# The convolution's sum leaves its PSUM bank through VectorE, half an image at a time, and 155 expert tiles run in place of 156

## What is computed

```python
def _L0_conv_ref(x, w1, b1, w2, b2, bias):
    avg = jnp.mean(x, axis=(2, 3))
    mx = jnp.max(x, axis=(2, 3))
    wt = softmax(((mx @ w2.T + b2) - (avg @ w1.T + b1)).reshape(b * c, 1, K, K), axis=1)
    y = conv_general_dilated(x, wt, feature_group_count=b * c) + bias
    return y + x
def _L0_ffn_ref(x, Wg, bg, W1, b1, W2, b2):
    top_w, top_i = top_k(xf @ Wg + bg, 2)
    w = softmax(top_w)
    for e in range(8):
        out += w[:, e] * (gelu(xf @ W1[e] + b1[e]) @ W2[e] + b2[e])
x = x + _L0_conv_ref(_ln_c(x), ...)
t = _to_tokens(x)
t = t + _L0_ffn_ref(_ln_t(t), ...)
```

## Time and profile before

| what | us |
|---|---|
| median of 3 runs | 1596.86 (1596.85 to 1596.99) |
| the profiled execution's span | 1597.2 |
| image phase, to the last routing row | about 570 |
| expert phase, first to last result | 625 to 1509 |
| last phase | 1510 to 1597 |

### The profile page before, as it was taken

The page is one execution under the profiler, slowest core; times in us unless marked ns, Lnnn a source line. Parts: engine busy times, 40 slices in busy tenths (PEclk is TensorE's granted clock), DMA queues, the critical chain, the costliest instruction groups (busy, mean ns, idle before and its releaser), DMA issues.

```text
span 1597.2 us, 45596 instructions
## 1 busy us (share of the span) xinstructions
PE 1476.3 (92%) x12254; PEld 1135.9 (71%) x12255; DVE 1379.2 (86%) x2725; ACT 1069.8 (67%) x2410; POOL 973.9 (61%) x1062
## 2 busy tenths in 40 slices
PE   5899999999998777999999999999999999999776
PEld 2344545454545426999999999999999999999654
DVE  2568888888888856999999999999999999999654
ACT  4577777777777415777777777777777777777400
POOL 1004556456545674777777777777777777777500
PEclk7999999999999757999999999999999999999866
DMA  4202122212121183111111111111111111110199
GB/s 136 80 27 67 60 76 66 68 58 79 62 69 50 41 141 74 43 44 44 47 47 45 42 38 47 44 47 41 47 47 41 49 43 47 47 44 8 39 403 399
DMA packets 62200, 115.77 MB, mean 72 GB/s; under 512 B 15551, under 2 KB 39259, under 8 KB 62154
## 3 DMA queue, kind: packets, MB, share of 16 engines
q1 hardware_dynamic: 37354, 62.28, 12.8%
q0 software_dynamic: 18176, 34.27, 6.9%
q10 hardware_dynamic: 6624, 18.69, 3.3%
HBM read 60.22 MB, written 58.61 MB: 74 GB/s over the span
## 4 chain that ended last, share of the span: by engine, by line
POOL 33%; issue 27%; PE 23%; ACT 7%; DMA 5%; DVE 3%; POOLq 1%; SPq 1%; ACTq 0%; DVEq 0%
POOL token_out L501 17%; PE psV L816 11%; POOL yt L496 7%; POOL xn L489 7%; DMA ye<-token_out 4%; PE psV L767 4%; ACT spent L597 3%; PE psT L801 2%; PE psA L758 2%; PE psG L803 2%; POOL rows_by_pair L471 2%; ACT cv L585 1%; ACT sq L553 1%; PE psV L995 1%; DMA stage<-in_L_ffn_W_dram 1%
## 5 line engine op out<-in xcount | busy, mean ns | idle before, releaser
L1309 DVE TENSOR_TENSOR gl<-g,gh 128x512 f16<-128x512 f32 x624 | 527.2, 884 | 13.3 <-ACT gh L701 6.2
L501 POOL DMA_INDIRECT token_out<-yt,rt x312 | 399.5, 1280 | 186.1 <-POOL yt L496 133.5
L471 POOL DMA_INDIRECT rows_by_pair<-rows,idx x256 | 271.7, 1061 | 322.0 <-issue 198.7
L816 PE MATMUL psV<-lp,diag 128*128 128x512 f32 x576 | 275.1, 610 | 18.7 <-ACT cv L585 17.6
L701 ACT ACTIVATE gh<-g 128x512 f16<-128x512 f32 x468 | 276.3, 624 | 17.2
L694 ACT ACTIVATE g<-psT 128x512 f32<-128x512 f32 x312 | 183.1, 597 | 107.3 <-DVE gl L1309 83.4
L694 ACT ACTIVATE g<-psV 128x512 f32<-128x512 f32 x312 | 185.1, 597 | 91.7 <-PE psV L935 80.7
L956 PE MATMUL psR<-wall,gh 128*128 x1248 | 222.7, 273 | 0.6 <-DVE ya L1326 0.6
L956 PE MATMUL psG<-wall,gh 128*128 x1248 | 222.7, 273 | 0.0
L957 PE MATMUL psG<-wall,gl 128*128 x1248 | 214.3, 219 | 0.0
L957 PE MATMUL psR<-wall,gl 128*128 x1248 | 214.3, 219 | 0.0
(11 more groups left out here) (210 smaller groups left out, 2951.6 us busy)
## 6 DMA issues: line engine op xcount, KB each, us to landing
rt<-rows_by_pair SPq DMA_DIRECT2D x156, 133.0 KB
xb<-in_x_dram SPq DMA_DIRECT2D x32, 512.0 KB, 3.5
ye<-token_out SPq DMA_DIRECT2D x32, 512.0 KB, 7.8
out_dram<-oe ACTq DMA_DIRECT2D x32, 512.0 KB, 8.5
token_out<-yt,rt POOLq DMA_INDIRECT x312
rows_by_pair<-rows,idx POOLq DMA_INDIRECT x256, 2.5
stage<-in_L_ffn_W_dram SPq DMA_DIRECT2D x1, 2048.0 KB, 8.6
rows_by_pair<-pad_rows SPq DMA_DIRECT2D x15, 133.0 KB
```

The source lines that it names most:

```text
L471: gp.indirect_dma_start(rows_dram, bass.IndirectOffsetOnAxis(ap=idx[p][:, b:b + 1].bitcast(U32), axis=0), rows[p][:, b, :], None).then_inc ...
L501: gp.indirect_dma_start(y_dram, bass.IndirectOffsetOnAxis(ap=rt[r][:, b, ID:ID + 1].bitcast(U32), axis=0), yt[r][:, b, :], None, bounds_ch ...
L816: ins = te.matmul(psConv.rearrange("p (h w) -> p h w", w=WW), diag[k][:, m, :], lp[j][:, y:y + HH // 2, dx:dx + WW], start=(m == 0), stop= ...
L1309: v.tensor_tensor(gl[side][q][:, cols], g[side][:, cols], gh[side][q][:, cols], ALU.subtract).then_inc(lo_done, 1)
```

## The change

`take` and the buffers `cv` are gone. `add_image` now works on half an image: it waits for the convolution's half (`conv_ready`), reads the bank, adds the bias (a value per partition) and the image in one instruction, writes half of `x1` and increments `cv_ready`, for which TensorE waits as before. The loads of images and the first `window` wait on `cv_ready` too, in place of `x_used`. There are four calls in a step where there were two: half 0 of image 0 behind `norm` 0, its half 1 where `add_image` 0 stood, half 0 of image 1 behind `norm` 1, and its half 1 where `add_image` 1 stood.

The number of tiles becomes the most that 32,768 tokens in 28 groups can need, (32768 + 28 * 255) // 256 = 155. As 155 is no multiple of 4 or 12, the written out end holds 7 tiles on TensorE and ScalarE (4 before) and 23 on VectorE and GpSimd (12 before); SyncE's loads of the last 11 tiles are written out.

```diff
-    NT = NTOK // T + NPAIR
+    NT = (NTOK + NPAIR * (T - 1)) // T
...
-        cv = [sb(f"cv{k}", [P, PIX], held=phase_a) for k in range(2)]
...
-                    sp.wait_ge(x_used, 4 * t + j + 1)
+                    sp.wait_ge(cv_ready, 8 * t + 2 * j + 2)
...
-            for j in range(NT - RING, NT):
+            for j in range(RING * (ROUNDS - 1), NT):
...
-            def take(st_, k, h):
-
-                act.wait_ge(conv_ready, st_.count(2, 4, 2 * k + h + 1))
-                if not st_.fixed or 2 * st_.t + st_.r > 1:
-                    act.wait_ge(x_used, st_.count(2, 2, k - 1))
-                sc_.activation(cv[k][:, h * HALF:(h + 1) * HALF], psConv, ACT.Identity, bias=conv_b[:, :], scale=1.0).then_inc(cv_ready, 1)
...
-            for j in range(NT - BODY, NT):
+            for j in range(BODY * (NT // BODY - 1), NT):
...
-            def add_image(st_, k):
-
-                j = 2 * st_.slot(2) + k
-                dve.wait_ge(cv_ready, st_.count(2, 4, 2 * k + 2))
-                v.tensor_tensor(x1[j][:, :], cv[k][:, :], xb[j][:, :], ALU.add).then_inc(x_used, 1)
+            def add_image(st_, k, h):
+
+                j, half = 2 * st_.slot(2) + k, slice(h * HALF, (h + 1) * HALF)
+                dve.wait_ge(conv_ready, st_.count(2, 4, 2 * k + h + 1))
+                v.scalar_tensor_tensor(out=x1[j][:, half], in0=psConv, scalar=conv_b[:, :], in1=xb[j][:, half],
+                                       op0=ALU.add, op1=ALU.add).then_inc(cv_ready, 1)
...
                 if st_.on(1):
                     norm(st_, 0)
+                if st_.on(2):
+                    add_image(st_, 0, 0)
...
-                    add_image(st_, 0)
+                    add_image(st_, 0, 1)
                     window(st_, 2, 0, 0, 2)
                 if st_.on(1):
                     norm(st_, 1)
+                if st_.on(2):
+                    add_image(st_, 1, 0)
...
-                    add_image(st_, 1)
+                    add_image(st_, 1, 1)
```

More of the change, by code:

```diff
@@ L101, in conv_moe_block @@
     AHEAD = 5
-    assert NT % RING == 0 and RING % BODY == 0 and BODY % 4 == 0
+    assert RING % BODY == 0 and BODY % 4 == 0 and ROUNDS > 2
     rows_dram = nc.dram_tensor("rows_by_pair", [NREG * CAP + T, RW], F32).ap()
@@ L188, in conv_moe_block @@
             sem, ("tap_ready", "z_ready", "ez_ready", "taps_ready", "diag_ready", "conv_ready"))
-        cv_ready, x_used, x1_ready = map(sem, ("cv_ready", "x_used", "x1_ready"))
+        cv_ready, x1_ready = map(sem, ("cv_ready", "x1_ready"))
         tok_ready, stat_ready, ssq_ready, tln_ready, rstd_ready, kept = map(
@@ L404, in _ @@
                 load_rows(first, r)
-            with sp.Fori(1, NT // RING, 1) as t:
+            with sp.Fori(1, ROUNDS, 1) as t:
                 for r in range(RING):
@@ L409, in _ @@
                     load_rows(first, r)
+            for j in range(RING * ROUNDS, NT):
+                first = sp.value_load(tab[0:1, 2 * j:2 * j + 1], min_val=0, max_val=NREG * CAP)
+                sp.wait_ge(y_out[j % RING], 16 * TB * ROUNDS)
+                load_rows(first, j % RING)
             for r in range(RING):
-                sp.wait_ge(y_out[r], 16 * TB * (NT // RING))
+                sp.wait_ge(y_out[r], 16 * TB * ((NT - 1 - r) // RING + 1))
             def load_e(t, j):
@@ L643, in step @@
                         high_b2()
-                    if st_.on(2):
-                        take(st_, k, 0)
                     if st_.on(1):
@@ L650, in step @@
                         keep(st_, k)
-                    if st_.on(2):
-                        take(st_, k, 1)
                     if st_.first and k == 0:
@@ L1099, in window @@
                     c_win.begin_at(st_.count(stage, len(taps_dve[0]) + len(taps_dve[1]) - 2, k * (len(taps_dve[0]) - 1)))
-                    dve.wait_ge(x_used, n + 1)
+                    dve.wait_ge(cv_ready, st_.count(stage, 4, 2 * k + 2))
                 for m in range(first, end):
```

## The result

The changed kernel takes 1621.22 us (median of 4 runs, 1620.00 to 1621.83), the kernel before 1596.92 us beside it (4 runs, 1596.85 to 1597.79). The ratio is 1.0148 [1.0134, 1.0162]: slower by some 24 us. The profiled execution has a span of 1619.0 us, 21.8 more than that of before.

The account below looks back on a forecast made before the run. The prediction took TensorE to bound the expert tiles and a loop of hand-overs the image phase. Terms 9.6 + 11.5 + 6.5 - 5.7 = 21.9 on 1597.2 gave 1619 us, range 1606 to 1624.

Parts of the forecast that it names:

- half 1, a step: First image's second half: its add stands behind the choice of experts, 0.80 us more in 12 steps, 9.6 us.
- half 2, a step: Second image's first half: its add queues behind the second norm, 0.82 us more in 14 steps, 11.5 us.
- Half 0: First image's first half: TensorE restarts within 0.1 us of before, VectorE's list behind moves by 0.70 us.
- The slack of 0.16: Ahead of the square: 0.16 us between centring and square, which cuts half 2's 0.98 us delay to 0.82.
- the removed copies return nothing: Copy ahead of the square, about 0.5 us on ScalarE, goes without gain because TensorE then arrives last, by 0.82 us.
- The tail: End of the image phase, step 16: 3.9 us later plus 2.6 us for a lower clock, 6.5 us together.
- over 4 us later: Sign in the changed profile: half 2 of step 16 starts over 4 us later against the end of step 15.
- the median of the runs is 0.3 below the profiled span: Step from span to time: median 1596.86 us is 0.3 below the profiled span, so 1619.1 became a forecast of 1619.
- Rival 1: Image phase: one of the two hand-overs, half 1's 9.6 or half 2's 11.5 us, is hidden; 1605 to 1610 us; chance 0.12.
- Rival 3: VectorE: the adds fit into its idle time, so only the tile counts; 1591 us; chance 0.05.
- rival 2: Ahead of the square: the copy's time comes back, 0.5 us in 14 steps, 7 us; 1584 us; chance 0.05.
- Rival 4: Steady image steps: TensorE's clock falls for 3 us a step, about 40 us more; 1660 us; chance 0.04.

Follow-up runs that it names:

- the run with half 3 alone: Kernel before with 155 tiles; VectorE adds only half 3 (second image's last) straight from the bank, ScalarE copies halves 0 to 2: 1591.29 us, ratio 0.9965.
- the two runs with one image each: Kernel before with 155 tiles, one image of a pair added straight from the bank, the other copied by ScalarE: first image straight 1612.11 us, second 1606.42 us.
- the pair of runs on place and load: Changed kernel with half 1's add between the two expert choices: 1606.42 us; kernel before, 155 tiles, one unused VectorE add per step ahead of first norm: 1591.46 us.
- both adds moved: Changed kernel with half 1's add between the two expert choices and half 2's ahead of the second norm: 1614.19 us, ratio 1.0107.
- the run with half 2's add alone moved: Changed kernel with half 2's add ahead of the second norm in place of behind it: 1626.89 us, ratio 1.019.
- the run with both adds moved and the early count: Both adds moved, and TensorE may begin half 0 when the first two of five diagonals are written: 1601.60 us, ratio 1.0025.

## Why the prediction was right

| term | predicted | measured |
|---|---|---|
| one add | 0.74 us | 0.746 |
| half 1, a step | 0.80 | 0.85 to 1.01, once 1.39 |
| half 2, a step | 0.82 | 0.78 to 0.82, once 0.43, once 1.41 |
| first `norm` to last | 9.6 + 11.5 + 0.8 (step 15) = 21.9 | 23.9 |
| behind the last `norm` | 6.5 - 0.8 = 5.7 | 4.5 |
| image phase | 27.6 | 28.4 |
| phase's end to the first expert result | 0 | -1.0 |
| expert tiles | -5.7 | -5.7 |
| span | +21.9 | +21.8 |

*Half 0* restarts 280.97 - 279.02 = 1.95 us after the `norm`, before 269.97 - 268.06 = 1.91: nothing, as said.

*Half 1* begins 291.03 - 279.02 = 12.01 us after it, before 279.27 - 268.06 = 11.21. That is the 0.80. The missing 0.10 is the restart: after an idle these four rows take 1.99 us, and took 1.88 without one. With it, the place loses 0.90 in this step. Over steps 3 to 15 it loses 12.4 us where 10.4 were forecast, and that is the whole 2 us by which the way from the first `norm` to the last came out longer; half 2 lost the 11.5 that were forecast.

*Half 2* gives TensorE the bank 297.36 - 295.40 = 1.96 us after the `norm` began; 1.94 was worked out. The slack of 0.16 held as well: in the run with half 3 alone the square came 0.17 us earlier and then waited for TensorE. That the removed copies return nothing shows in ScalarE's rows; the square is released by the centring:

```profile
270.30 1.02 ACT L556 ACTIVATE sq<-psA 128x1024 f32<-128x1024 f32 x1 [1.26 <-PE psA L750]
```

*The tail* has the shape that was worked out, with two sizes off. VectorE and TensorE in step 16, behind the earlier trace rows:

```profile
557.29 0.75 DVE L1085 SCALAR_TENSOR_TENSOR x<-psV,conv_b,xb 128x512 f32<-128x512 f32 x1
```

```profile
548.11 4.56 PE L808 MATMUL psV<-lp,diag 128*128 128x512 f32 x10 [0.91 <-DVE x L1085]
...
558.18 5.37 PE L808 MATMUL psV<-lp,diag 128*128 128x512 f32 x8 [3.27 <-DVE x L1085]
```

```profile
556.00:560.00 4.00, 1.82 (x3) 0.97 (x4) 3.76 (x11) 2.56 (x15) 0.50 (x1) 0.83 0.05 17
560.00:564.00 4.00, 4.00 (x12) 1.63 (x10) 1.02 (x2) 2.16 (x8) 0.00 (x0) 0.74 0.00 0
```

The idle is 3.27 us (3.3 predicted). Half 2 starts 558.18 - 528.75 = 29.43 us after the last `norm`, before 530.92 - 504.88 = 26.04: 3.4 late, of 3.6 predicted (the sign "over 4 us later" had counted step 15's half 1 in). Its rows take 5.37 us in place of 3.68, so the lower clock cost 1.7 and not 2.6: it fell only within the matmuls, not to the level of the earlier trace rows for all of them. Together the tail is 1.2 us shorter than predicted, which hides half of the 2 us by which the steps are longer. The rest is hidden by the 1.0 us behind the phase, for which the prediction had no term; by the scatter of that way its sign is luck. So the sum is closer than its terms: errors of 0.1 to 2 us cancel in it, and a span that is right to 0.1 us is luck.

*The step that failed* is the last: "the median of the runs is 0.3 below the profiled span". A time is not below its own span. The profiled execution of the changed kernel took 1620.96 us with a span of 1619.0, and every run of this study took 1.7 to 3.0 us more than its own span. The profile of before was of a slower execution than the timed ones. The span was forecast to 0.1 us, the time came out 2.2 above the forecast.

*The rivals.* Rival 1 falls by the two runs with one image each. Rival 3 falls by the pair of runs on place and load. For rival 2, the bank had to be free as early as before; in the kernels run here that doesn't come without a later `norm`, and the one copy that was removed without delay, half 3's, gave 1.2 us over 14 steps, 2.0 once the taps' chain gave way too. The Trainium skill, "ScalarE: Activation LUTs", Rules for kernel authors, puts additions on VectorE; the trace agrees on the work (746 ns against 683 plus half of 1.23 us), and the time disagrees because of the list's order. Rival 4 is real, but in another kernel. Its 40 us took 3 us at the lower clock for 3 us lost; the 2.15 us of the earlier trace rows would make it 30, and the three steps with both adds moved lost 2.0 to 2.7 each.

## What to carry to other kernels

Moving work to an engine with idle time costs what stands ahead of it in that engine's list at the moment its data is ready: here 0.5 us more of work a step cost 28.6 us, and 0.75 us in a gap cost none. Before a step of a chain is shortened, look for a second chain that ends at the same instruction; here two met, in part of the steps, some 11.8 us behind the same `norm`. In those steps shortening either alone gave nothing; where the second chain ended 0.26 us earlier, shortening the first gave 0.18 us.

## What the runs showed of the hardware that was not expected

TensorE's clock fell to 1.2 GHz within looped steps, in the one shown after idles of 0.26 and 1.27 us, in three steps of the run with both adds moved and one of the run with half 2's add alone moved. It did not fall in the looped steps of the changed kernel, which idles 0.58 and 1.18 and more in each, nor in those of the run with both adds moved and the early count, with idles of 0.26 and 1.29 us in the step shown. What decides between them isn't shown here. The new add took 746 ns with a scalar operand read from SBUF; the same operation with a constant takes 680.
